# Scores and values of the second context stage as products of 32 held columns on four column groups

## The chip, the cores and the metric

The kernel runs on one core of a Trainium2 chip. The metric is the device time of one execution in microseconds: three runs of the kernel before gave a median of 1007.44 us (1006.71 to 1007.72). One further execution was taken with the hardware profiler; times "from the span's start" are of that one.

A core has a matrix engine (PE, with its weight loads shown apart as PEld), a vector engine (DVE), a scalar engine (ACT), a general engine (POOL) and a queue for transfers and waits (SP). A matrix instruction holds one operand in the array (the held columns, up to 128) and moves the other through it. A held operand of 32 columns whose output starts at partition 0, 32, 64 or 96 takes one of four column groups of the array.

## The reference, cut to what matters

Eight sequences of 100 rows, 512 wide, pass two decoder layers: self-attention, cross-attention over a context of 722 rows for each sequence, and a feed-forward part, each followed by a layer norm. The change is in the second layer's cross-attention:

```
q = x @ Wq.T + bq;  k = ctx @ Wk.T + bk;  v = ctx @ Wv.T + bv
scores = einsum('bqh,bkh->bqk', q, k) * SCALE
attn = softmax(scores, axis=1)                 # over the 100 queries
out = einsum('bqk,bkh->bqh', attn, v) @ Wo.T + bo
```

The softmax runs over the queries, so with keys on partitions and queries along the free axis it is a row-wise operation.

## The kernel before, in words

The program is a chain of stages, each a block in which every engine has its own list of instructions, tied together by semaphores; the order on each engine is the order in which the code emits. The weights of the second cross-attention are folded beforehand, so that in this stage the scores are products of the 512-wide context itself with a 512-wide query `qT`, and the values are products of the context with the softmax; what is left of `Wv` and `Wo` comes in the next stage, which begins behind a barrier of all engines (L1507).

`context_columns` (L1491) is the stage of the change. It goes over the eight sequences b ("context rows" here). The 722 keys are six tiles, five of 128 and one of 82 (`PARTS`, `keys`); the 512 columns are four chunks (C = 4), T = 100 queries, P = 128, HD = 32.

On PE, `scores(b)` (L1519) forms for each key tile j and chunk k one fp32 product: 128 (or 82) keys held, 100 queries moving, added up over k in one bank for the first five tiles and in another for the last: 24 products. `value(b, c)` (L1531) forms for each chunk c six products over the key tiles, 128 columns of the context held, 100 queries moving: 24 products for the four chunks. Behind the last chunk stand six products with a held tile of ones, 32 columns wide, on column groups in turn (L1548): the sums of the softmax weights. The order is scores(0), and then for each b scores(b + 1) and the four value(b, c).

DVE adds the bias and takes the maxima (`shift`, L1587), and after ACT's exponential (`expo`, L1562) sums, inverts and scales (`share`, L1604). The order is shift(b + 1), share(b + 1), one piece of another job (`beside`: rounding the last stage's kernel to fp8, L2874 and L1184 to L1190) and `count(b)`, which copies the sums. ACT copies the values (`keep_a`, L1569). POOL adds a bias to x at the start of the stage.

SP loads for each b from 2 on the context row as it is (L794, L796) into a ring of five buffers, waits until the scores of b - 2 are done, and loads the turned context of b (L2505, from a scratch tensor written in the first layer) into one of two buffers. The first two of each are loaded ahead of the stage.

Of the kernel before, what the change touches and what calls it, by code (L numbers as in the profile page):

```python
# [23 lines left out]
P = 128  # L24
B, T, D = 8, 100, 512
S = 722
NH, HD = 16, 32
C = D // P
# [3 lines left out]
KT = -(-S // P)  # L32
# [82 lines left out]
def program(nc, g, out):  # L115
    ctx = ExitStack()
    with ctx:
        def sb(name, shape, dt=F32, where=ctx):
            return where.enter_context(nc.sbuf_tensor(name, shape, dt))
# [4 lines left out]
        def sb_at(name, shape, offset, dt=F32):  # L124

            return nc.alloc_sbuf_tensor_at(name, shape, dt, offset=offset)
# [13 lines left out]
        ps = ctx.enter_context(nc.psum_tensor("ps", [P, 8, 512], F32))  # L140
# [380 lines left out]
        raw = [sb_at(f"l0_raw{i}", [P, C, D], shelf_at + 4 * C * D * i) for i in range(3)]  # L521
# [262 lines left out]
        RAWS = 5  # L784
# [387 lines left out]
        qT = sb_at("x0_qT", [P, C, N], qk_at)  # L1172
# [21 lines left out]
        SB, VB = 3, 7  # L1194
        keys = lambda j: P if j < KT - 1 else LAST
# [295 lines left out]
        def context_columns(name, qT, aT_out, scale, phase, sums_out, qbk, rows_landed, beside):  # L1491
# [4 lines left out]
            raw = raws  # L1496
            ct = turned_ahead
            pk = sb(name + "_pk", [P, 2, KT, T], F32, phase)
            pT = sb(name + "_pT", [P, 2, KT, T], F32, phase)
# [7 lines left out]
            with nc.Block() as block:  # L1507
                @block.sync
                def _(sp):
                    for b in range(2, B):  # L1510
                        if b >= RAWS:
                            sp.wait_ge(used, b - RAWS + 1)
                        load_context(sp, 1, b)
                        sp.wait_ge(scored, 2 * (b - 1))
                        load_turned(sp, b)

                @block.tensor
                def _(pe):
                    def scores(b):  # L1519
                        if b >= 1:  # L1520
                            pe.wait_ge(shifted, 2 * b)
                        pe.wait_ge(came[b % 2], 16 * (b // 2 + 1))
                        for i, rows_, j0, j1 in PARTS:
                            for j in range(j0, j1):
                                for k in range(C):
                                    mm = nc.tensor.matmul(ps[0:rows_, SB + i, (j - j0) * T:(j - j0 + 1) * T],  # L1526
                                                          ct[b % 2][:, k, j * P:j * P + rows_], qT[:, k, b * T:(b + 1) * T],
                                                          start=k == 0, stop=k == C - 1, skip_group_check=True)
                            mm.then_inc(scored, 1)

                    def value(b, c):  # L1531
                        if c == 0:
                            pe.wait_ge(even, b + 1)
                            pe.wait_ge(landed[b % RAWS], 32 * (b // RAWS + 1))
                            if b >= 1:
                                pe.wait_ge(a_kept, b)
                        for j in range(KT):
                            mm = nc.tensor.matmul(ps[:, VB, c * T:(c + 1) * T],  # L1538
                                                  raw[b % RAWS][0:keys(j), j, c * P:(c + 1) * P],
                                                  pT[0:keys(j), b % 2, j, :], start=j == 0, stop=j == KT - 1,  # L1540
                                                  skip_group_check=True)
                        if c == C - 1:
                            mm.then_inc(used, 1)
                            if b >= 1:
                                pe.wait_ge(counted, b)
                            for j in range(KT):
                                group = j % HPC
                                mm = nc.tensor.matmul(ps[group * HD:(group + 1) * HD, 5, 0:T], one[0:keys(j), :],  # L1548
                                                      pT[0:keys(j), b % 2, j, :], start=j < HPC, stop=j + HPC >= KT,
                                                      skip_group_check=True)  # L1550
                            mm.then_inc(summed, 1)

                    scores(0)
                    for b in range(B):
                        if b + 1 < B:
                            scores(b + 1)
                        for c in range(C):
                            value(b, c)
# [939 lines left out]
        qT = sb_at("x1_qT", [P, C, N], qf_at)  # L2498
# [617 lines left out]
```

## Time and profile before

| what | value |
|---|---|
| median of three runs | 1007.44 us |
| the profiled execution: span from first to last instruction | 1003.7 us (its own whole time isn't on the page; what lies around the span is taken as the 3.7 us to the median) |
| PE / PEld busy | 934.0 / 757.2 us |
| DVE / ACT / POOL busy | 429.3 / 346.5 / 250.9 us |
| scores L1526, passes and busy time | 384, 46.4 us |
| values L1538, passes and busy time (two groups: shelf, ctx_lent) | 288 and 96, 33.2 and 11.0 us |

One page shows one execution. A busy time is the union of the instructions of an engine; matmuls are pipelined, so the time between two starts, and not the length of one, is its price. What ends an engine's idle time is named behind an arrow. Instruction packets are the program's code on its way to an engine.

### The profile page before, as it was taken

The page shows a single profiled execution, that of the slowest core. Times are in us where ns is not written, and L with a number is a line of the kernel's source. Part 1 is how long each engine was busy: PE and PEld are TensorE (multiplying, and loading weights), DVE is VectorE, ACT ScalarE, POOL GpSimd, SP SyncE. Part 2 cuts the span into 40 slices and gives each one's busy share as a digit, 9 for nine tenths or more (in the row PEclk, how much of TensorE's full clock was granted, in tenths as well). Part 3 has the DMA queues.
Part 4 walks back from the last instruction along what each step waited for, and adds up shares of the span by engine and source line. Part 5 has one row for each costly group of instructions (what it writes and reads, how often), then busy time and mean ns, then how long its engine had stood idle before and what let it go on. Part 6 is the DMA issues. An engine that isn't in the chain of part 4 may idle for free. (4 is left out here: it accounts for less than half of the span.)

```text
span 1003.7 us, 19227 instructions
## 1 busy us (share of the span) xinstructions
PE 934.0 (93%) x7747; PEld 757.2 (75%) x7747; DVE 429.3 (43%) x994; ACT 346.5 (35%) x886; POOL 250.9 (25%) x306
## 2 busy tenths in 40 slices
PE   5999999989998889999999999999889899999994
PEld 5977776676775644789999999987765578999532
DVE  2973454224442647002112132135267630656576
ACT  2322323245552124122222233324276611122374
POOL 5452111023554306000000010004065403000275
PEclk9999999999999979899999999997969998999996
DMA  9994000245622807259999888700040032971001
GB/s 254 382 331 127 2 2 2 98 152 203 238 120 95 309 7 254 55 181 386 358 383 313 284 269 283 254 29 28 4 153 3 2 119 78 321 247 66 1 15 51
DMA packets 72456, 162.01 MB, mean 161 GB/s; under 512 B 4132, under 2 KB 5685, under 8 KB 70321
## 3 DMA queue, kind: packets, MB, share of 16 engines
q1 hardware_dynamic: 70048, 156.54, 45.8%
q0 software_dynamic: 2320, 4.25, 1.4%
q8 instruction: 61, 1.00, 0.4%
q14 instruction: 27, 0.21, 0.1%
HBM read 128.81 MB, written 31.97 MB: 160 GB/s over the span
## 5 line engine op out<-in xcount | busy, mean ns | idle before, releaser
L2113 PE MATMUL ps<-ffn_h,ffn_w 128*128 128x128 f32 x1280 | 149.1, 275 | 0.0
L2113 PEld LDWEIGHTS ps<-ffn_h,ffn_w 128*128 128x128 f32 x1280 | 145.9, 192 | 0.0
L2113 PE MATMUL ps<-ffn_xh,ffn_w 128*128 128x128 f32 x640 | 74.9, 275 | 0.3 <-ACT ffn_xh L2147 0.3
L2203 DVE TENSOR_SCALAR ffn_h<-ps,tile_bias 128x128 f32<-128x128 f32 x80 | 22.5, 345 | 122.4 <-PE ps L2113 122.4
L2113 PEld LDWEIGHTS ps<-ffn_xh,ffn_w 128*128 128x128 f32 x640 | 73.1, 192 | 0.9 <-issue 0.9
L1418 POOL TENSOR_TENSOR ctx_low<-shelf,ctx_high 128x1024 fp32r<-128x1024 f32 (+2 forms) x24 | 43.0, 1819 | 65.4 <-PE ps L1283 33.7
L2161 ACT ACTIVATE ffn_y<-ffn_y 128x128 f32<-128x128 f32 x80 | 23.7, 298 | 73.9 <-DVE ffn_y L2219 73.9
L1526 PE MATMUL ps<-x_qT,ctx_ct 128*128 128x100 f32 (+1 forms) x384 | 46.4, 284 | 2.3 <-PEq L137 2.0
L1526 PEld LDWEIGHTS ps<-x_qT,ctx_ct 128*128 128x128 f32 (+1 forms) x384 | 45.0, 197 | 3.7 <-issue 3.2
L2219 DVE SCALAR_TENSOR_TENSOR ffn_y<-ps,tile_bias,ffn_gate_row 128x128 f32<-128x128 f32 x80 | 22.6, 344 | 58.0 <-PE ps L2113 57.9
L2834 POOL TENSOR_TENSOR att_e<-att_e,decay 100x400 f32<-100x400 f32 x32 | 32.7, 1033 | 46.1 <-DVE att_e L2685 46.1
L111 PE MATMUL ps<-ctx_ct,x_qT 128*100 128x210 f32 (+1 forms) x128 | 40.3, 467 | 1.0 <-DVE ctx_ct L1432 0.7
L2155 ACT ACTIVATE ffn_h<-ps,tile_bias 128x128 f32<-128x128 f32 x80 | 22.8, 368 | 41.6 <-PE ps L2113 41.6
L3007 POOL TENSOR_TENSOR rstd<-rstd,minus_half 100x1 f32<-100x1 f32 x16 | 11.6, 740 | 99.6 <-DVE rstd L2950 95.0
L111 PEld LDWEIGHTS ps<-ctx_ct,x_qT 128*100 128x100 f32 x128 | 20.6, 166 | 18.7 <-issue 17.4
L2781 ACT ACTIVATE att_e<-att_e,att_mx 100x100 f32<-100x100 f32 x96 | 28.1, 365 | 15.5 <-DVE att_mx L2690 15.5
L1538 PE MATMUL ps<-ctx_pT,shelf 128*128 128x100 f32 (+1 forms) x288 | 33.2, 275 | 0.2 <-ACT xf L1571 0.2
L1538 PEld LDWEIGHTS ps<-ctx_pT,shelf 128*128 128x128 f32 (+1 forms) x288 | 32.6, 192 | 0.4 <-issue 0.4
L1565 ACT ACTIVATE ctx_pk<-ctx_pk,ctx_st 128x100 f32<-128x100 f32 x48 | 13.8, 365 | 54.9 <-DVE ctx_st L1601 54.9
L2906 PE MATMUL ps<-x_n,xf 128*100 128x512 f32 x64 | 29.9, 596 | 0.6 <-PEq L1507 0.6
L111 PE MATMUL ps<-l_ro,xf 128*100 128x512 f32 x64 | 29.7, 608 | 0.0
L2147 ACT ACTIVATE ffn_xh<-ps 128x512 f32<-128x512 f32 x20 | 11.8, 598 | 49.1 <-PE ps L2074 49.1
(469 smaller groups left out, 2096.8 us busy)
## 6 DMA issues: line engine op xcount, KB each, us to landing
ffn_w<-in_L_ffn_w_dram SPq DMA_DIRECT2D x60, 1024.0 KB, 6.0
shelf<-in_ctx_dram SPq DMA_DIRECT2D x12, 1280.0 KB
expert_rows<-nothing SPq DMA_DIRECT2D x1, 14820.0 KB, 49.6
context_turned<-ctx_ct SPq DMA_DIRECT2D x8, 1444.0 KB, 7.9
ctx_ct<-context_turned SPq DMA_DIRECT2D x8, 1444.0 KB, 12.5
ctx_lent<-in_ctx_dram SPq DMA_DIRECT2D x4, 1280.0 KB
rows_own<-expert_rows SPq DMA_DIRECT2D x8, 260.0 KB, 3.0
x_wo<-in_L_xattn_Wo_dram SPq DMA_DIRECT2D x1, 2048.0 KB, 9.5
```

Source lines behind the costliest of these rows:

```text
L111: last = pe.matmul(out, a, b, start=(n == 0), stop=(n == len(products) - 1))
L1418: nc.gpsimd.tensor_tensor(raw_low[b % RAWS][0:rows_, j0:j1, :], raw[b % RAWS][0:rows_, j0:j1, :], raw_high[b % 2][0:rows_, j0:j1, :].bitca ...
L1526: mm = nc.tensor.matmul(ps[0:rows_, SB + i, (j - j0) * T:(j - j0 + 1) * T], ct[b % 2][:, k, j * P:j * P + rows_], qT[:, k, b * T:(b + 1) * T],
L1538: mm = nc.tensor.matmul(ps[:, VB, c * T:(c + 1) * T], raw[b % RAWS][0:keys(j), j, c * P:(c + 1) * P], pT[0:keys(j), b % 2, j, :], start=j ...
L2113: mm = nc.tensor.matmul(acc(n)[:, m, :], w[:, n % SLOTS, k, m * P:(m + 1) * P], into[l][:, i % 2, k, :], start=k == 0, stop=k == C - 1, sk ...
L2155: nc.scalar.activation(h1[:, i % 2, m, :], acc(n)[:, m, :], ACT.Relu, bias=bsel[:, m, i, 0:1]).then_inc(h1_kept, 1)
L2161: nc.scalar.activation(y[:, i % 2, m, :], y[:, i % 2, m, :], ACT.Relu, accum_out=vT[:, m, i:i + 1]).then_inc(counted, 1)
L2203: nc.vector.tensor_scalar(h2[:, i % 2, m, :], acc(n)[:, m, :], bsel[:, m, i, 1:2], 0.0, ALU.add, ALU.max).then_inc(h2_kept, 1)
L2219: nc.vector.scalar_tensor_tensor(y[:, i % 2, m, :], acc(n)[:, m, :], bsel[:, m, i, 2:3], gate_row[:, i % 2, :], ALU.add, ALU.mult).then_in ...
L2781: ins = nc.scalar.activation(e[:, c, :], e[:, c, :], ACT.Exp, bias=mx[:, b % 2, r, c:c + 1])
L2834: nc.gpsimd.tensor_tensor(e, e, decay[:, :].unsqueeze(1).to_broadcast([T, C, T]), ALU.mult).then_inc(faded, 1)
L2906: mm = nc.tensor.matmul(ps[0:T, b % 3, :], xf[:, k, b * T:(b + 1) * T], n1[:, k, :], start=k == 0, stop=False)
```

## The change

In `scores` each product of up to 128 held keys is split into products of 32 held keys (the last of a tile of 82 has 18), each writing its own 32 partitions of the same bank. In `value` each product of 128 held columns is split into four of 32. The moving operand, the sums over k or j, the waits and the semaphores stay as they are; the semaphore is raised by the last of the products.

```diff
--- before.py
+++ after.py
@@ -1523,9 +1523,11 @@
                         for i, rows_, j0, j1 in PARTS:
                             for j in range(j0, j1):
                                 for k in range(C):
-                                    mm = nc.tensor.matmul(ps[0:rows_, SB + i, (j - j0) * T:(j - j0 + 1) * T],
-                                                          ct[b % 2][:, k, j * P:j * P + rows_], qT[:, k, b * T:(b + 1) * T],
-                                                          start=k == 0, stop=k == C - 1, skip_group_check=True)
+                                    for lane in range(0, rows_, HD):
+                                        end = min(lane + HD, rows_)
+                                        mm = nc.tensor.matmul(ps[lane:end, SB + i, (j - j0) * T:(j - j0 + 1) * T],
+                                                              ct[b % 2][:, k, j * P + lane:j * P + end], qT[:, k, b * T:(b + 1) * T],
+                                                              start=k == 0, stop=k == C - 1, skip_group_check=True)
                             mm.then_inc(scored, 1)
 
                     def value(b, c):
@@ -1535,10 +1537,11 @@
                             if b >= 1:
                                 pe.wait_ge(a_kept, b)
                         for j in range(KT):
-                            mm = nc.tensor.matmul(ps[:, VB, c * T:(c + 1) * T],
-                                                  raw[b % RAWS][0:keys(j), j, c * P:(c + 1) * P],
-                                                  pT[0:keys(j), b % 2, j, :], start=j == 0, stop=j == KT - 1,
-                                                  skip_group_check=True)
+                            for lane in range(0, P, HD):
+                                mm = nc.tensor.matmul(ps[lane:lane + HD, VB, c * T:(c + 1) * T],
+                                                      raw[b % RAWS][0:keys(j), j, c * P + lane:c * P + lane + HD],
+                                                      pT[0:keys(j), b % 2, j, :], start=j == 0, stop=j == KT - 1,
+                                                      skip_group_check=True)
                         if c == C - 1:
                             mm.then_inc(used, 1)
                             if b >= 1:
```

## Rows read from the trace of the kernel before

**Rows 1.** Page, busy time, share of the span and instructions of each engine.

```profile
PE 934.0 (93%) x7747; PEld 757.2 (75%) x7747; DVE 429.3 (43%) x994; ACT 346.5 (35%) x886; POOL 250.9 (25%) x306
```

**Rows 2.** Table by windows: length, then busy us (instructions) per engine, clock, DMA share, GB/s.

```profile
core 0: us, PE busy (x) PEld busy (x) DVE busy (x) ACT busy (x) POOL busy (x), PEclk, DMA share, GB/s
861.95:873.00 11.05, 11.05 (x110) 10.90 (x108) 6.42 (x17) 2.12 (x8) 0.00 (x0) 1.00 0.97 324
842.50:850.40 7.90, 7.90 (x47) 7.77 (x46) 0.52 (x1) 0.00 (x0) 7.90 (x8) 0.61 0.53 187
```

**Rows 3.** PE's timeline, one context row: start, length, line, tiles, shape, count.

```profile
861.48 0.54 PE L1548 MATMUL ps<-ctx_pT,ctx_one 128*32 128x100 f32 x12
861.95 5.39 PE L1526 MATMUL ps<-x_qT,ctx_ct 128*128 128x100 f32 x48
867.18 5.52 PE L1538 MATMUL ps<-ctx_pT,shelf 128*128 128x100 f32 x48
872.64 0.54 PE L1548 MATMUL ps<-ctx_pT,ctx_one 128*32 128x100 f32 x12
```

**Rows 4.** Timeline of all engines, the stage's first and second scores on PE.

```profile
841.83 8.62 PE L1526 MATMUL ps<-x_qT,ctx_ct 128*128 128x100 f32 x48 [1.97 <-PEq L137]
...
850.80 5.39 PE L1526 MATMUL ps<-x_qT,ctx_ct 128*128 128x100 f32 x48 [0.35 <-DVE ctx_pk L1593]
```

**Rows 5.** PE's timeline in the two attentions, and the window of L2587's 32 passes.

```profile
158.13 0.90 PE L907 MATMUL ps<-att_aT,l_v 100*32 100x100 f32 x32
158.84 0.87 PE L913 MATMUL ps<-att_aT,picks 100*32 100x100 f32 x32
...
737.88 1.56 PE L2587 MATMUL ps<-att_aT,l_v 100*32 100x100 f32 x32 [0.59 <-ACT att_aT L2793]
739.21 1.56 PE L2593 MATMUL ps<-att_aT,picks 100*32 100x100 f32 x32
...
737.88:739.21 1.33, 1.33 (x32) 1.33 (x36) 0.24 (x1) 1.33 (x5) 1.33 (x2) 0.50 0.49 160
```

**Rows 6.** Timeline, DVE behind the last scores.

```profile
922.47 0.94 DVE L1593 TENSOR_TENSOR ctx_pk<-ps,x_qbk 128x500 f32<-128x500 f32 x2 [2.45 <-PE ps L1526]
...
927.26 0.78 DVE L1613 TENSOR_TENSOR ctx_pT<-ctx_pk,ctx_st 128x600 f32<-128x600 f32 x1
...
933.69 0.43 DVE L1190 SCALAR_TENSOR_TENSOR kernel<-k_quant 128x256 bf16<-128x256 f32 x1
...
935.25 0.26 DVE L1619 COPY x_sums<-ps 128x100 f32<-128x100 f32 x1 [1.13 <-PE ps L1548]
```

**Rows 7.** SP's timeline, first and fifth of five; then DMA issues, median us to landing.

```profile
850.48 0.33 SPq L2505 DMA_DIRECT2D ctx_ct<-context_turned  x1
...
889.69 0.33 SPq L2505 DMA_DIRECT2D ctx_ct<-context_turned  x1
...
ctx_ct<-context_turned SPq DMA_DIRECT2D x6, 1444.0 KB, 12.8
```

**Rows 8.** Table by windows, a loaded spell and the time behind the last.

```profile
868.80:877.00 8.20, 8.20 (x82) 7.95 (x81) 4.64 (x12) 2.12 (x7) 0.00 (x0) 1.00 0.96 318
906.60:917.00 10.40, 10.40 (x97) 10.40 (x96) 5.84 (x15) 1.83 (x7) 0.00 (x0) 1.00 0.09 35
```

**Rows 9.** Page's DMA queues (packets, MB, share); windows between packets; queues, 899.4 to 900.0.

```profile
q8 instruction: 61, 1.00, 0.4%
...
886.40:899.40 13.00, 13.00 (x127) 12.75 (x126) 6.69 (x17) 2.23 (x7) 0.00 (x0) 1.00 0.86 273
...
899.40:908.70 9.30, 9.30 (x94) 9.05 (x93) 6.37 (x16) 2.22 (x7) 0.00 (x0) 1.00 0.53 193
...
q8 instruction: 1, 0.02, 12.8%
```

**Rows 10.** Window from the last q8 packet to the end; DMA queues, 937.6 to 1003.7.

```profile
936.98:1003.70 66.72, 49.62 (x165) 21.93 (x163) 43.24 (x98) 38.06 (x72) 36.38 (x54) 0.86 0.09 25
...
q1 hardware_dynamic: 880, 1.64, 8.7%
q14 instruction: 1, 0.01, 0.0%
```

## The prediction

> **What bounds the kernel now.** The page's busy shares come first: PE has 93% of the span, DVE 43%, ACT 35% [rows 1]. Next the table by windows, for the stage itself. In a steady context row PE has no idle time at all, DVE works 6.4 of 11 us, the clock is 1.00 and the DMA share is high [rows 2]; yet after 906.6 us, with a DMA share of 0.09, PE is just as full [rows 8]. So neither DVE nor the memory sets the pace; PE does. PE's timeline gives the period: sums at 861.48, the next at 872.64, 11.16 us, made of 0.47 us of sums, 48 score passes from 861.95 to 867.18 (5.23 us, 109 ns each) and 48 value passes to 872.64 (5.46 us, 114 ns each) [rows 3]. There are 24 products in each 48: one fp32 product is two passes, and each pass has a weight load of its own. The first 48 score passes took longer, 841.83 to 850.80 with a wait of 0.35 us, 8.62 us [rows 4], at a clock of 0.61, mostly the lower level [rows 2].
>
> The span is 1003.7 us, the median of the runs 1007.44; the 3.7 us between lie around the program's instructions. All sums below are differences, set against that median.
>
> **The products.** The new instruction holds 32 columns and still moves 100. The trace has such a thing: L907 in the first attention holds 32 columns on four column groups in turn, and its 32 passes and the next line start 0.71 us apart [rows 5], 22.2 ns each, 89 ns for four. So four new passes take 89 ns where one old one took 109 to 114. The upper bound is L1548 of this stage, the same form on 128 rows: 12 passes in 0.47 us [rows 3], 39 ns each, 157 ns for four. Its six products on four groups leave two groups empty half of the time and its start is in it, so L907, 32 passes in a row, is nearer. The lower bound would be a perfect overlap, an old pass cut to a quarter; then DVE is the floor, with 5.57 us of work on the scores (922.47 to 928.04), 2.91 us of rounding and 0.26 us of copying a row [rows 6], 8.7 us. At a clock of 0.50, the 1.2 GHz level, L2587 takes 1.33 us for 32 passes, 166 ns for four [rows 5].
>
> Per context row: scores are 20 products on four groups and 4 on three (82 keys: 32, 32, 18), which I price like four: 48 x 89 ns = 4.27 us. Values the same, 4.27 us. With the sums 9.0 us instead of 11.16. Over the stage: first scores 48 x 166 ns = 8.0 us, -0.6; seven further scores 7 x -0.96 = -6.7; eight values 8 x -1.19 = -9.5. Together -16.8 us for PE alone. At the upper bound of 157 ns each row's 96 groups of four cost 96 x 68 ns = 6.5 us more than at 89 ns, 52 us in all, +35 us net.
>
> **What is late next.** Three covers are used up.
>
> DVE: behind the last scores it has 5.57 us of work on them and then two pieces of rounding with their copies, 11.9 us, of which some 0.7 us start before the scores end; that is 11.2 [rows 6]. PE's tail goes from 2 x 5.93 = 11.9 us to 9.5. So 1.7 us of the gain stay there.
>
> Memory: SP issues the turned row b when the scores of b - 2 are done, and context row b + 1 behind it; landing takes 12.8 us [rows 7]. At 9.0 us a period there are 2 x 9.0 - 4.3 = 13.7 us. The traffic fills the DMA engines for 8.2 us of a period [rows 8]. Both just fit; I allow 0.4 us. So far -16.8 + 1.7 + 0.4 = -14.7 us.
>
> Code: this is the cost that the edit doesn't mention. The page has 61 instruction packets on q8, 1.00 MB, 16.4 KB each [rows 9], and 15,494 PE and PEld instructions [rows 1]: 254 a packet. A context row had 48 x 4 + 24 = 216 of them; now its scores are 92 part products and its values 96, with 4 instructions each, and 24 for the sums: 776. The stage goes from 1,728 to 6,208 instructions, from 7 packets to 24, and at 9.0 us a row a packet is used up in 2.97 us instead of 13.
>
> How soon does one come? Packets start at 886.4, 899.4 and 908.7. Between the first two 127 + 126 instructions start, between the others only 94 + 93 [rows 9]. The one at 899.4 is asked for while the memory is loaded, the one at 908.7 while it is quiet [rows 8]. So the loaded one comes 66 instructions later against the same place in the code, at 216 in 11.16 us some 3.4 us. The packet itself takes 12.8% of 16 engines x 0.6 us = 1.2 us [rows 9]. From asking to landing: at least 4.6 us loaded, 1.2 us quiet. And how much is in hand? Behind the packet of 936.98 none follows on q8, and 165 + 163 instructions still start [rows 10]. Less its own 256, some 70 of the program were in store when it came (and what the trace doesn't show of the end). So PE runs one block while the next is fetched, and has no longer reserve.
>
> The Trainium skill (Runtime: NRT & Kernel Launch, Instruction fetch mechanics) has the next block of 256 instructions fetched while the current one runs, calls the cost mostly hidden, and gives TensorE a store of 2048 instructions. The block size agrees with the packets here; the depth disagrees with the 328 instructions behind the last one. By that rule the sum stops at -14.7 us, which is the first rival.
>
> With one block in hand, PE waits where a block takes 4.6 us to come and 2.97 us to run. In a period with traffic, 8.2 loaded us let 8.2 / 4.6 = 1.8 blocks through, and the other 1.2 of its 3.03 blocks (776 / 256) run at 2.97: 11.8 us at most. The wait that is open when the traffic ends is cut short, by up to 3.4 us and by 1.7 us on average: 10.1 us. I take 11.2, nearer to the upper end, since a turned row still trickles after the spell (12.8 us to land against 8.2). Five pairs of transfers are issued, 850.48 to 889.69 [rows 7], so five periods cost 5 x 2.2 = 11 us over 9.0: -14.7 + 11 = -3.7 us. With 10.1 it is -9.2, with 11.8 it is -0.7. Forecast: 1007.4 - 3.7 = **1003.7 us**, its own range 998 to 1008.
>
> **The rivals.**
> *Code comes in time.* If a block is asked for earlier than I read, nothing stalls: 1007.4 - 14.7 = 992.7 us. For it: no view puts an idle time of PE down to code, though four-group bursts stand in both attentions [rows 5]. Against it: such a burst, 64 MATMULs, is half a block.
> *Code comes later still (slower).* The place is the same queue. If the packet goes through an engine that works off the tail of a turned row, the loaded spell lasts the 12.8 us to landing, not 8.2: 12.8 / 4.6 = 2.8 blocks, then 0.25 x 2.97, 13.5 us a period, 5 x 4.5 = 22 us back: +8 us, 1015 us. It decides from a mean block time of 11.16 / 3.03 = 3.7 us on. For it: the landing time. Against it: the packet of 908.7 came soon while the last turned row still landed. A clock at half in the stalls adds little where code is late (a block then takes 32 x 166 ns = 5.3 us), and more in the quiet rows.
> *The groups don't overlap* as in L907, since all four share one moving tile and add up in place: at L1548's pace +35 us, 1042 us, and code hides behind that. Against it: L1548's 39 ns hold a start and two empty groups.
>
> **Numbers.** A measurement of this kernel can tell 0.2%, 2.0 us, from no change. Forecast 0.47 (0.32 of it faster by more than that, 0.11 within, 0.04 slower); code in time 0.26, all faster; code later still 0.21, of which 0.01 within; no overlap 0.06, of which 0.03 is a product only a little dearer than 89 ns that ends within. Faster 0.58, same 0.15, slower 0.27. The range takes in the first two rivals to their centres: 992 to 1016.
>
> **What would show it.** Right: 32 passes at full clock start within some 0.71 us; 17 more packets on q8; gaps in PE within a run of L1526 or L1538, with no engine as releaser, that end when a packet has landed, and only while the DMA share is near 1; rows after the last transfer at 9.0 us; DVE's last copy ends the stage. The first step is wrong if four passes take over 100 ns. The step on code is wrong if the loaded rows run at 9.0 us (then 993), or if gaps stand in the quiet rows too (then 1015 and more).

## The result and the profile after

The changed kernel takes 1023.49 us (median, 1021.06 to 1023.99) beside 1007.08 us (1005.55 to 1007.72) for the kernel before on the same chip: ratio 1.0173, 95% interval 1.0153 to 1.0193. It is slower by 16.4 us; forecast were 3.7 us faster. The time lies outside the range given (992 to 1016), on the side of the rival "Code comes later still".

The page first: busy times, the two groups of the change, the queue of instruction packets.

```profile
PE 922.8 (91%) x9987; PEld 739.8 (73%) x9987; DVE 430.8 (42%) x994; ACT 347.2 (34%) x886; POOL 251.3 (25%) x306
...
q8 instruction: 79, 1.29, 0.5%
...
L1528 PE MATMUL ps<-x_qT,ctx_ct 128*32 128x100 f32 (+1 forms) x1472 | 39.7, 257 | 19.8 <-issue 17.4
...
L1541 PE MATMUL ps<-ctx_pT,shelf 128*32 128x100 f32 (+1 forms) x1152 | 31.1, 263 | 8.9 <-issue 8.4
```

PE works 11 us less than before [rows 1], and yet the kernel is longer: PE has got idle time in the very lines that were changed (19.8 and 8.9 us), and what ends it is "issue": the profile shows no engine and no transfer of data that PE waited for. The table of waits for the stage (840 to 960 us) has the sums:

```profile
PE ps L1528 <- issue: 17.4, 12, 4.6
...
PE ps L1541 <- issue: 8.8, 9, 3.2
```

Together 26.2 us in 21 waits. PE's timeline shows where; up to 911.68 in rows with transfers, from 934.62 in one without (start, length, line, tiles, count, idle time before it):

```profile
858.67 5.56 PE L1541 MATMUL ps<-ctx_pT,shelf 128*32 128x100 f32 x128 [3.19 <-issue]
...
890.67 1.67 PE L1541 MATMUL ps<-ctx_pT,shelf 128*32 128x100 f32 x68 [0.82 <-issue]
...
892.54 1.25 PE L1528 MATMUL ps<-x_qT,ctx_ct 128*32 128x100 f32 x42
897.12 3.03 PE L1528 MATMUL ps<-x_qT,ctx_ct 128*32 128x100 f32 x128 [3.33 <-issue]
900.59 0.45 PE L1528 MATMUL ps<-x_qT,ctx_ct 128*32 128x100 f32 x9 [0.44 <-issue]
...
904.15 1.83 PE L1541 MATMUL ps<-ctx_pT,ctx_lent 128*32 128x100 f32 x74 [0.45 <-issue]
...
911.68 5.03 PE L1528 MATMUL ps<-x_qT,ctx_ct 128*32 128x100 f32 x141 [4.56 <-issue]
...
934.62 2.95 PE L1528 MATMUL ps<-x_qT,ctx_ct 128*32 128x100 f32 x128 [0.32 <-issue]
938.09 0.80 PE L1528 MATMUL ps<-x_qT,ctx_ct 128*32 128x100 f32 x23 [0.52 <-issue]
...
941.65 2.17 PE L1541 MATMUL ps<-ctx_pT,shelf 128*32 128x100 f32 x90 [0.44 <-issue]
```

From 897.12, and again from 934.62, exactly 128 MATMULs stand before the next gap, with their weight loads 256 instructions: one packet, called a block here. From 934.62 the 128 start within 2.70 us, and behind the first four each further four take 86 ns. PE stops at the end of nearly every block, in the quiet row too. Behind 911.68 it doesn't: the granted clock is at 0.50 from 912.3 to 915.7, and three blocks (383 recorded MATMULs) follow each other without an idle time, up to the gap ahead of 924.17. The next table is cut at the starts of packets on q8, as the trace's DMA records have them (us, busy times, clock, DMA share, GB/s):

```profile
887.97:894.63 6.66, 5.00 (x213) 4.64 (x204) 4.55 (x12) 2.24 (x7) 0.00 (x0) 1.00 0.95 343
894.63:898.25 3.62, 1.13 (x52) 1.13 (x56) 0.60 (x3) 0.00 (x0) 0.00 (x0) 1.00 0.50 184
898.25:901.82 3.57, 3.13 (x144) 2.91 (x135) 1.29 (x3) 0.00 (x0) 0.00 (x0) 1.00 0.03 11
901.82:909.25 7.43, 4.85 (x210) 4.40 (x201) 5.24 (x14) 2.24 (x7) 0.00 (x0) 1.00 0.93 331
...
928.85:932.32 3.47, 3.03 (x141) 2.80 (x133) 1.64 (x3) 1.73 (x6) 0.00 (x0) 1.00 0.04 9
932.32:935.75 3.43, 3.11 (x139) 2.89 (x132) 3.16 (x10) 0.51 (x1) 0.00 (x0) 1.00 0.02 5
```

A packet follows the last after 3.4 to 3.6 us where the memory is quiet, and after 6.7 and 7.4 us where the DMA share is 0.95 and 0.93, against the 2.7 us that a block takes to run. Over the whole stage, five spacings of packets have a DMA share of over 0.9, and they are 6.3 to 7.4 us. Timeline and table together show which part of the fetch grows. From a packet's start to PE's next start it is 2.30 us in the quiet row (932.32 to 934.62), and 2.70 and 2.43 us in loaded rows (887.97 to 890.67, 909.25 to 911.68). From there to the next packet's start it is 1.13 us in the quiet row (934.62 to 935.75), but 3.96 and 5.10 us behind a burst (890.67 to 894.63, 904.15 to 909.25). So the traffic puts off the start of the packet. The late packets are those that fall into a burst of SP, its loads of a turned and a context row:

```profile
887.24 0.33 SPq L2508 DMA_DIRECT2D ctx_ct<-context_turned  x1
887.61 0.44 SPq L794 DMA_DIRECT2D shelf<-in_ctx_dram  x1
...
901.17 0.33 SPq L2508 DMA_DIRECT2D ctx_ct<-context_turned  x1
```

The stage's account, from the first score to the next stage's first MATMUL: 94.0 us before (841.83 to 935.83), 106.8 after (844.53 to 951.34). By the starts of the sums (L1548 before, L1551 after):

| stretch | before | after | difference |
|---|---|---|---|
| stage's start to first sums | 19.65 | 21.87 | +2.2 |
| the first five periods | 55.8 | 66.6 (11.96, 13.78, 13.61, 15.15, 12.08) | +10.8 |
| the sixth period | 11.15 | 10.61 | -0.5 |
| last values, and to the next stage | 7.4 | 7.7 | +0.3 |

The last of the five periods is nearly without transfers (a DMA share of 0.09, as in the kernel before [rows 8]); its long gap, 1.92 us ahead of 924.17, follows a packet that came 5.2 us after the one before it, behind the last turned row.

That is 12.8 of the 15.6 us between the two spans (1003.7 and 1019.3). The other 2.7 us lie ahead of the stage, where no code differs. In the fourteen profiles of this case the stage starts between 839.9 and 846.6 us. Where it starts by 841.9, its first scores run wholly or in part at a clock of 0.50, as in the profile before; where it starts from 843.7 on, they run at 1.00, as in the profile after. So both the later start and the faster first scores go with the execution and not with the change.

The 3.7 us that were taken to lie around the program's instructions are too many: in the runs that have both numbers, the time is 1.7 to 2.9 us above the span. No difference above rests on them.

### The profile page after: what moved, and what is told of

The parts are those of the page before. It is cut to its first block and busy times, and to the rows that moved or that the text cites. A ratio compares the mean times of both kernels' runs of the same rounds, so it can differ in the third digit from the quotient of the medians.

```text
span 1019.3 us, 23707 instructions
## 1 busy us (share of the span) xinstructions
PE 922.8 (91%) x9987; PEld 739.8 (73%) x9987; DVE 430.8 (42%) x994; ACT 347.2 (34%) x886; POOL 251.3 (25%) x306
## 5 line engine op out<-in xcount | busy, mean ns | idle before, releaser
L1528 PE MATMUL ps<-x_qT,ctx_ct 128*32 128x100 f32 (+1 forms) x1472 | 39.7, 257 | 19.8 <-issue 17.4
L1528 PEld LDWEIGHTS ps<-x_qT,ctx_ct 128*32 128x32 f32 (+1 forms) x1472 | 35.6, 113 | 23.0 <-issue 22.4
L1541 PE MATMUL ps<-ctx_pT,shelf 128*32 128x100 f32 (+1 forms) x1152 | 31.1, 263 | 8.9 <-issue 8.4
L1541 PEld LDWEIGHTS ps<-ctx_pT,shelf 128*32 128x32 f32 (+1 forms) x1152 | 28.2, 117 | 11.1 <-issue 10.1
L1568 ACT ACTIVATE ctx_pk<-ctx_pk,ctx_st 128x100 f32<-128x100 f32 x48 | 13.9, 368 | 63.7 <-DVE ctx_st L1604 63.7
```

What stands on the lines that cost most here:

```text
L1528: mm = nc.tensor.matmul(ps[lane:end, SB + i, (j - j0) * T:(j - j0 + 1) * T], ct[b % 2][:, k, j * P + lane:j * P + end], qT[:, k, b * T:(b ...
L1541: mm = nc.tensor.matmul(ps[lane:lane + HD, VB, c * T:(c + 1) * T], raw[b % RAWS][0:keys(j), j, c * P + lane:c * P + lane + HD], pT[0:keys( ...
```

## The experiments

The theory was the instruction fetch: a block comes later than it is used up, and later still under transfers. The rivals were that the four groups themselves stall, and that the transfers slow the passes. All ratios are to the kernel before on the same chip.

**e1_noload4 and e8_noload128: the transfers of the stage taken out**, in the four-group form and in the form before. With the loads go PE's waits for the later ones.

```diff
-                    for b in range(2, B):
...
-                        load_context(sp, 1, b)
-                        sp.wait_ge(scored, 2 * (b - 1))
-                        load_turned(sp, b)
+                    sp.wait_ge(used, B)
```

> Leaves out the twelve loads of context rows and turned rows inside the stage; every context row is computed from the first two, so the output is not the reference's, but PE's instructions are those of the changed kernel. Code theory: PE waits for its own code, and a block of 256 instructions takes about 3.5 us from one to the next when the memory is quiet and 6 to 7 us when it is loaded. Without loads every row runs at 776/256 x 3.5 = 10.6 us, no gap of PE is longer than about 1 us, the stage is 8 x 10.6 = 85 us plus the start, some 8 us under the stage before, and the time falls to 998 to 1003 us. Rival (the column groups themselves stall PE, by switching groups or adding up four groups in one bank): the gaps don't care for the loads, and the time stays at 1020 to 1024 us.

Measured: 1004.88 us, ratio 0.9990 [0.9976, 1.0004]. The timeline of the same stretch:

```profile
886.36 3.03 PE L1523 MATMUL ps<-x_qT,ctx_ct 128*32 128x100 f32 x128 [0.86 <-issue]
890.11 0.45 PE L1523 MATMUL ps<-x_qT,ctx_ct 128*32 128x100 f32 x9 [0.71 <-issue]
...
894.22 1.83 PE L1536 MATMUL ps<-ctx_pT,shelf 128*32 128x100 f32 x74 [1.00 <-issue]
...
897.90 3.11 PE L1523 MATMUL ps<-x_qT,ctx_ct 128*32 128x100 f32 x128 [0.72 <-issue]
```

The gaps of 3 to 4.6 us are gone, and with them the 1.7%: the transfers make them. But a gap of 0.5 to 1.1 us stands at nearly every block: from gap to gap it is 3.85 us (886.36 to 897.90, three blocks), without any load from outside. The gaps add up to 15.0 us. So the quiet fetch alone takes the whole gain, and the time is 2 us above what the code theory expected, since it had taken 3.5 us for the quiet fetch. Why it is 3.85 here and 3.5 in the changed kernel is open; the profile is of an execution 3.3 us above the median.

> The kernel before without the twelve loads inside the stage; every row is computed from the first two, so the output is not the reference's. Code theory: 216 instructions a row need a block every 13 us, which comes in time with and without traffic, so rows stay at 11.15 us and the time within 0.2% of the kernel before. Rival (the traffic slows PE's passes themselves, by the memory that both use): rows under 11.0 us and a time 2 us or more under the kernel before; then part of what the changed kernel gained without loads is not code.

Measured: 1005.58 us, ratio 0.9996 [0.9986, 1.0007]; the periods are 11.16 us:

```profile
862.25 0.54 PE L1543 MATMUL ps<-ctx_pT,ctx_one 128*32 128x100 f32 x12
862.72 5.39 PE L1521 MATMUL ps<-x_qT,ctx_ct 128*128 128x100 f32 x48
867.95 5.52 PE L1533 MATMUL ps<-ctx_pT,shelf 128*128 128x100 f32 x48
873.41 0.54 PE L1543 MATMUL ps<-ctx_pT,ctx_one 128*32 128x100 f32 x12
```

Transfers don't slow the passes of 128 columns; they slow the fetch.

**e3_scores4 and e4_values4: each half of the change alone.** e3 has the changed scores and the values of before, e4 the reverse.

> Only the scores as four products of 32; the values as before. 488 instructions a row. Code theory: a block lasts on average 256/488 x 10.2 = 5.4 us; within the scores 368 instructions follow at 11 ns each, so one or two gaps a row, in the scores alone, up to 3.5 us where the memory is loaded and under 0.6 us where it is quiet; 1006 to 1013 us. Rival (groups stall PE): half of the loss, 1013 to 1017 us, with the same gaps in quiet and in loaded rows.

> Only the values as four products of 32; the scores as before. 504 instructions a row. Code theory: as for the scores alone, gaps in the values only; the transfers start at the end of the scores, so the values are where the memory is loaded, and the loss is at least that of the scores alone: 1007 to 1015 us. Rival (groups stall PE): half of the loss, 1013 to 1017 us.

Measured: e3 1005.04 us, 1.0003 [0.9985, 1.0021], below both theories' ranges; e4 1010.32 us, 1.0049 [1.0024, 1.0074], as expected of code. The first fence is e3, the second e4.

```profile
881.68 4.34 PE L1528 MATMUL ps<-x_qT,ctx_ct 128*32 128x100 f32 x182
885.96 5.60 PE L1540 MATMUL ps<-ctx_pT,shelf 128*128 128x100 f32 x48
...
891.80 4.34 PE L1528 MATMUL ps<-x_qT,ctx_ct 128*32 128x100 f32 x182
```

```profile
882.99 3.54 PE L1539 MATMUL ps<-ctx_pT,shelf 128*32 128x100 f32 x153
890.38 1.73 PE L1539 MATMUL ps<-ctx_pT,shelf 128*32 128x100 f32 x36 [3.85 <-issue]
```

e3's steady periods are 10.1 to 10.4 us without a gap: 184 passes on four groups in 4.3 us, at a DMA share of 0.79. That refutes the rival of stalling groups. The values of before, 192 instructions in 5.5 us, leave a pause in which the fetch can catch up. e3's loss stands at its start in this profile (gaps of 1.13 and 2.60 us ahead of 853.57 and 860.00, and a clock at 0.50 from 859.3 to 873.0 us). But the profile is of one of three executions that took 1009.4 to 1010.5 us; the other seven took 1003.4 to 1005.6, and no trace shows what takes the gain of the steady periods in those. In e4 the burst of code comes right after the scores, when SP has just issued its loads, and the gaps are there (11.4 us in five waits); its profile too is of the slowest of ten executions, 7.3 us above the median. The halves cost 0.0% and 0.5% and together 1.7%. That with both halves no slow stretch is left fits this, and isn't shown by a run of its own.

**e7_scores4_late: the four-group scores from b = 2 on only**, to spare e3's start. The edit is shown against e3.

```diff
-                                    for lane in range(0, rows_, HD):
-                                        end = min(lane + HD, rows_)
+                                    wide = HD if b >= 2 else P
+                                    for lane in range(0, rows_, wide):
+                                        end = min(lane + wide, rows_)
```

> Four products of 32 for the scores of rows 2 to 7 alone; the scores of rows 0 and 1, which follow each other at once, and all values as before. Code theory: 368 instructions of scores fall where the last transfer has ended, and 120 of values and sums where the next runs; no gaps, rows of 10.1 to 10.4 us, and none of the two long gaps that the scores of row 1 and the first values had with the scores alone. 6 x -0.95 = -5.7 us against the kernel before, 998 to 1001 us. Rival (what was lost at the start of the stage is not code but the slow clock there): no better than with all scores, 1003 to 1006 us.

Measured: 1005.74 us, 0.9997 [0.9982, 1.0012]: no better, and in the range of the rival. Whether by its reason, the slow clock at the start, isn't settled: in this profile the first scores are those of the kernel before, 8.62 us at half clock. Gaps of 1.98 and 1.02 us now stand inside the scores, in loaded periods (ahead of 875.88 and 898.29). Fewer instructions ahead shift the ends of blocks against the rows. That their place within the burst decides is a reading of this one profile, and it wasn't foreseen.

**e2_two, e5_two_even, e6_two_single: two groups of 64 columns.** Half as many instructions. In e2 the last tile's 82 keys go as 64 and 18, in e5 as 32, 32 and 18, in e6 as one product. The edit is that of e6; e5 has HD in the place of the last P, and e2 has 2 * HD throughout.

```diff
-                                    for lane in range(0, rows_, HD):
-                                        end = min(lane + HD, rows_)
+                                    wide = 2 * HD if rows_ == P else P
+                                    for lane in range(0, rows_, wide):
+                                        end = min(lane + wide, rows_)
...
-                            for lane in range(0, P, HD):
+                            for lane in range(0, P, 2 * HD):
```

> Two products of 64 held columns on two column groups in place of four of 32: 408 instructions a context row in place of 776, with the same work. Code theory: if two 64-column passes overlap (89 ns for the pair, as four of 32), a block lasts 256/408 x 9.0 = 5.6 us, more than the 3.5 us of a quiet fetch, so quiet rows run at 9.0 us without a gap; a loaded fetch of 6 to 7 us leaves short gaps, about 10.3 us a loaded row. Five rows at -0.9, three at -2.1, +1.7 for DVE's tail: about -9 us, 996 to 1000 us, faster than both kernels. Rival (the groups themselves stall PE): half of the additional passes, so about half of the loss, 1013 to 1017 us. If 64-column groups don't overlap, a pair takes 166 ns and the time is over 1045 us.

Measured: 1002.09 us, 0.9966 [0.9955, 0.9978], faster than both kernels, but 2.1 us above the range. No gap for code is left:

```profile
869.03 5.88 PE L1528 MATMUL ps<-x_qT,ctx_ct 128*64 128x100 f32 x96
874.84 4.35 PE L1541 MATMUL ps<-ctx_pT,shelf 128*64 128x100 f32 x96
879.12 0.54 PE L1551 MATMUL ps<-ctx_pT,ctx_one 128*32 128x100 f32 x12
```

The values' 96 passes take 4.28 us to the next line, 89 ns a pair: a pair of 64 costs what four of 32 cost. The scores' 96 take 5.81 us. The records of single passes put the excess into the last tile, where 64 and 18 columns take turns: a pass behind such a change starts 179 ns after the one before it, and a pair of 64 takes 86 ns. Not every change of width costs this: in e5 a pass of 18 columns starts 7 ns after one of 32.

> Two groups of 64 for the values and the five full key tiles, three groups of 32, 32 and 18 for the tile of 82 keys, so that the width of the groups changes once before that tile and once behind it and not with every product. 424 instructions a row. Theory on widths (a change between groups of 64 and of 32 columns costs a start of 180 ns in place of 86): the scores fall from 5.6 us, as with 64 and 18 in turn, to 3.4 + 0.7 + 0.2 = 4.3 us; a row without traffic takes 9.0 to 9.3 us. Code theory: a block lasts 256/424 x 9.2 = 5.6 us, a quiet fetch of 3.5 to 3.9 us is hidden, a loaded one of 6 to 7 leaves gaps of up to 1 us, rows of 9.6 to 10.4 us. Together 995 to 999 us, faster than all so far. Rival to the widths (the 82 keys themselves, or adding up two groups in one bank): the scores stay at 5.6 us and the time at 1002. Rival to the code theory: no gaps in loaded rows, 9.2 us throughout, 993 us.

> As the run with two even groups, but the tile of 82 keys is one product as before the change. 392 instructions a row. Theory on widths: the last tile takes 8 x 112 = 0.9 us and two changes of width, about 0.3 us a row more than three groups of 32; code theory: a block lasts 6.0 us, so shorter gaps in loaded rows. 996 to 1000 us.

Measured: e5 1001.31 us, 0.9950 [0.9932, 0.9967]; e6 1001.39 us, 0.9946 [0.9927, 0.9966]. Without the turns the scores take 4.4 us, as expected, but both times are 1.4 to 2.3 us above the range: another wait takes over (in e5 there are also four gaps for code, 2.4 us). In e6's timeline, of PE and then of SP:

```profile
902.87 0.54 PE L1552 MATMUL ps<-ctx_pT,ctx_one 128*32 128x100 f32 x12
906.72 6.15 PE L1529 MATMUL ps<-x_qT,ctx_ct 128*64 128x100 f32 x88 [3.31 <-DMA ctx_ct<-context_turned]
```

```profile
888.89 3.65 SPq L2509 DMA_DIRECT2D ctx_ct<-context_turned  x1
892.58 0.57 SPq L794 DMA_DIRECT2D shelf<-in_ctx_dram  x1
893.19 3.53 SPq L796 DMA_DIRECT2D shelf<-in_ctx_dram  x1
898.69 5.81 SPq L2509 DMA_DIRECT2D ctx_ct<-context_turned  x1
```

With code out of the way PE waits for turned rows (6.4 us in four waits), and behind the longest the clock is at 0.50 from 907.0 to 910.4. The turned row, wanted at once, stands behind a context row that is wanted a period later; the next runs test whether that is the cause.

**e9 to e12: the order of SP's loads**, in e6's form and, as controls, in the kernel before. e9 and e10 issue context rows two ahead; e11 and e12, whose edit this is, issue the turned row ahead of the context row:

```diff
+                        if b == 2:
+                            load_context(sp, 1, b)
+                        sp.wait_ge(scored, 2 * (b - 1))
+                        load_turned(sp, b)
+                        if b > 2:
                             if b >= RAWS:
                                 sp.wait_ge(used, b - RAWS + 1)
                             load_context(sp, 1, b)
-                        sp.wait_ge(scored, 2 * (b - 1))
-                        load_turned(sp, b)
```

> Two groups of 64 with the last tile as one product, and SP issues context rows two ahead and the turned row right behind the scores of two before. If the remaining loss of the two-group form is the late turned row (waits of the scores on it: 6.4 us in three places in the run without this), the rows come down to 9.2 to 9.6 us without that wait, and the time is 993 to 998 us. If the transfers themselves are the bound (a period can't be shorter than what the two loads of a row take), the wait only moves to the context row or stays, and the time is 1000 to 1002 us as without the new order.

> The kernel before with that same order of loads on SP, as a control. PE's rows are 11.15 us and never wait for a load, so both theories expect no change: 1004 to 1007 us, within 0.2% of before. If the order of the loads itself brings or costs time, it shows here.

Measured: e9 1005.19 us, 0.9992 [0.9976, 1.0008]; e10 1011.75 us, 1.0063 [1.0044, 1.0081]. Both missed: the first turned row now has two context rows in front of it and a third right behind. In e9 PE waits 5.61 us for it, and 3.8 us in three later places. In e10, on the kernel before:

```profile
860.33 0.54 PE L1552 MATMUL ps<-ctx_pT,ctx_one 128*32 128x100 f32 x12
865.22 7.85 PE L1530 MATMUL ps<-x_qT,ctx_ct 128*128 128x100 f32 x48 [4.36 <-DMA ctx_ct<-context_turned]
```

4.36 us of waiting and scores of 7.85 instead of 5.39 us (the clock is at 0.50 from 863.6 to 870.4): 6.8 us in one place, though every other period is 11.15 us.

> Two groups of 64, last tile as one product, and the turned row b issued ahead of context row b (from b = 3 on), so that it no longer stands behind 1.4 MB that is needed 14 us later. If the late turned row is an order of transfers, its waits (6.4 us in the run without this) fall to under 2 us, most rows run at 9.2 to 10.2 us, and the time is 994 to 999 us. If the rows are bound by the bytes themselves (2.9 MB a row at 324 GB/s are 9.0 us, with nothing to spare at 9.2), the wait stays, on the turned or on the context row, and the time is 1000 to 1003 us.

> The kernel before with this order of loads, as a control: PE's rows of 11.15 us hide either order, so both theories expect 1004 to 1007 us, within 0.2% of before, and no wait on a turned row.

Measured: e11 **995.89 us, 0.9905 [0.9891, 0.9919]**, the best version; e12 1004.90 us, 0.9998 [0.9986, 1.0009]. In e11:

```profile
868.53 0.54 PE L1555 MATMUL ps<-ctx_pT,ctx_one 128*32 128x100 f32 x12
869.00 4.50 PE L1532 MATMUL ps<-x_qT,ctx_ct 128*64 128x100 f32 x88
873.43 4.35 PE L1545 MATMUL ps<-ctx_pT,shelf 128*64 128x100 f32 x96
877.71 0.54 PE L1555 MATMUL ps<-ctx_pT,ctx_one 128*32 128x100 f32 x12
...
924.38 3.65 PE L2913 MATMUL ps<-x_n,xf 128*100 128x512 f32 x8 [1.70 <-PEq L1507]
```

The time lies in the range that the order of the loads gave, and e12 is unchanged, as expected. A period is 9.18 us, in four of six; one wait of 1.5 us for a turned row and one gap of 0.74 us for code are left. The stage takes 79.9 us, and at its end PE waits 1.70 us at the barrier.

## Why the prediction was wrong

**Price of a pass: right.** 86 ns for four at full clock against 89 forecast. What the change brings per pass reads differently, though, once the tile of 82 keys is looked at by itself in the kernel before:

```profile
866.58 0.76 PE L1526 MATMUL ps<-x_qT,ctx_ct 128*82 128x100 f32 x7
867.18 0.50 PE L1538 MATMUL ps<-ctx_pT,shelf 128*128 128x100 f32 x3
```

Seven passes of 82 columns and the next line start 0.60 us apart, 86 ns each; the records of single passes put those of 128 columns 112 ns apart. The 109 ns of the prediction is the mean of both, with the start of the first pass in it. So a narrower pass already has the price of four groups without any split, and the groups bring 26 ns for each pass of 128 columns and nothing for the tile of 82. The Trainium skill (TensorEngine Tiling (Array Packing), Key Properties) has the tiles of the array load weights and multiply independently of each other, and has a change of the tiling mode drain the engine. The 86 ns for four passes, the price of one pass of 82 columns, agree with the first; e2's 179 ns starts agree with the second.

**Packets, blocks, one in hand: right.** 18 more packets (17 forecast), gaps that end with code and stand 256 instructions apart. Only the sign "only while the DMA share is near 1" was wrong, since the quiet rows have gaps too. The page that the prediction weighed (the Trainium skill, Runtime: NRT & Kernel Launch, Instruction fetch mechanics) calls the cost mostly hidden. The traces agree at 216 instructions a row, as in e8, and, but for one gap of 0.74 us, at 392, as in e11; they disagree at 776.

**"How soon does one come?": this step failed.** It put "at least 4.6 us loaded, 1.2 us quiet", and the sum used both as if they were the values. Measured are 6.3 to 7.4 us loaded and 3.4 to 3.6 us quiet. The difference that was read from the packets [rows 9], 3.4 us, was right (6.66 - 3.57 = 3.1 and 7.43 - 3.57 = 3.9); the base under it was not. Two intervals give only a difference, and for the base the packet's own 1.2 us was put in, with nothing for asking and for starting. The quiet row shows both: 2.30 us from the packet's start to PE's, and 1.13 us from there to the next packet's start, together 3.43. It fits this that a fetch begins only when the block before it has begun to run.

**From this the size follows.** A quiet block was "hidden" in 2.97 us and takes 3.5, so the quiet period is 3.03 x 3.5 = 10.6 us (10.61 measured, 9.0 forecast). A loaded period has one block in the burst and two outside: 6.66 + 2.03 x 3.55 = 13.9 us (13.78 and 13.61 measured, 11.2 forecast). The term "five loaded periods" was 11 us over 9.0; measured are 66.6 - 45 = 21.6 us, 10.6 more, and the quiet period adds 1.6. The sum also had no code term ahead of the first sums, where gaps of 1.19, 3.19 and 0.92 us stand: it had 8.0 + 0.35 + 2 x 4.27 = 16.9 us there, and measured are 21.9. These three make 17.2 us; the whole stage is 16.5 us above the 90.3 us that the sum gives it (94.0 - 3.7). The text had named the sign, "if gaps stand in the quiet rows too (then 1015 and more)", but gave that rival 0.21; its mechanism, the 12.8 us to landing, isn't what was seen: packets between bursts come in 3.6 us.

**First scores.** Forecast at half clock, -0.6 us. In this execution they ran at full clock, 4.32 us against 8.62 [rows 4], which is luck of the execution, as the starts of the stage show. In or right behind two of the longest gaps the clock fell to half instead (857.6 to 864.5 and 912.3 to 915.7), and 128 passes from 858.67 took 5.56 us, against 2.95 from 934.62. How far the two cancel isn't shown.

**DVE's tail and memory.** In the changed kernel neither shows, since code is later. Both are real once it isn't: e11's barrier waits 1.70 us (0.63 in e12), and the turned rows cost e6 6.4 us. The 0.4 us for memory was too little at that pace.

**What stays open.** The profiles put 12.8 us in the stage, the spans differ by 15.6 and the medians by 16.4. The 2.8 us outside the stage are the two executions' own, and so are some us inside it, by the clock of the first scores. In the medians, e1's 0.9990 against 1.0173 puts some 18 us down to the transfers. No run shows why a packet starts late behind a burst: whether it waits in a queue or for the memory.

## What to carry to other kernels

Before a product is split, divide the stage's instructions by 256 and compare a block's run time with the spacing of packets in a stretch where PE really stops for code; a spacing seen while code is in time tells how fast blocks are used, not how fast they can come. Take the fewest groups that still overlap and keep their width the same from pass to pass: two of 64 were worth what four of 32 were, at half the code, and the tile of 82 keys needed no split. When an engine gets faster, look again at the order of the loads: the one wanted first must not stand behind one wanted a period later.

## What the runs showed of the hardware

- Where PE stopped for code, a block of 256 instructions came every 3.4 to 4.1 us with a quiet memory (the changed kernel and e1), and every 6.3 to 7.4 us where the DMA share was over 0.9; what grew was the time from a block's start to the next packet's, from 1.1 us to 4.0 and 5.1. 128 passes of 32 columns (2.7 us) outrun it.
- Moving 100 columns, two passes on groups of 64 held columns cost 86 ns together, four on groups of 32 cost 86, one of 82 columns 86, and one of 128 columns 112. A pass behind a change between 64 and 18 columns starts 179 ns after the last, one behind a change from 32 to 18 starts 7 ns after.
- At a DMA share of 0.97 [rows 2] or without the stage's transfers (e8), passes of 128 columns keep a period of 11.15 us to 0.01 us.
